# A graph-network kernel on one core: the adjacency build's table of chunk ranges goes from one packed word a block to three plain words

## The reference, cut to what matters

```python
def reference(x, src, dst, edge_attr_8, edge_type_2, edge_weight, ...):
    ei = jnp.stack([src, dst])
    x = ln(x + L0(x, ei, edge_weight))   # segment_sum over ei[0] of (x @ W)[ei[1]] * edge_weight, + bias
    x = ln(x + L1(x, ei, edge_type_2))   # two relational layers, weights mixed from 30 bases, gated
    x = ln(x + L2(x, ei))                # degree-normalized sum over neighbours
    x = ln(x + L3(x, ei, edge_attr_8))   # attention over the edges, 8 heads, bias edge_attr_8
    return x
```

## Time and profile before

| | |
|---|---|
| median of 3 runs | 1315.63 us (1310.06 to 1317.89) |
| the profiled execution | 1321.34 us |
| its span (first to last instruction) | 1319.6 us |
| mean granted clock of PE in it, as a share of full speed | 0.981 |
| PE busy | 1223.5 us (93%) |
| DVE busy | 862.3 us (65%) |
| ACT busy | 419.5 us (32%) |
| POOL busy | 309.3 us (23%) |
| build, first to last matmul of L1600 | 68.7 to 245.9 us |

### The profile page before, as it was taken

One profiled execution on the slowest core, in us unless ns is written; L12 is line 12 of the kernel. 1 busy time (PEld: TensorE's weight loads), 2 busy tenths in 40 slices (PEclk: granted clock), 3 DMA queues, 4 the chain that ended last, 5 costly groups with the idle time before them and its releaser, 6 DMA issues.

```text
span 1319.6 us, 22145 instructions
## 1 busy us (share of the span) xinstructions
PE 1223.5 (93%) x8447; PEld 551.8 (42%) x8448; DVE 862.3 (65%) x1178; ACT 419.5 (32%) x564; POOL 309.3 (23%) x220
## 2 busy tenths in 40 slices
PE   6888888899898999999999999989999899999997
PEld 2233333333343333344445443444332455555553
DVE  7475666344334555462478873646999788879787
ACT  2444555322232111212301002125551343334332
POOL 2011010000010243453555655555560000000000
PEclk9988999999998999999999999989999899999999
DMA  8577885598696888745122212113221665556552
GB/s 305 207 235 237 278 288 181 208 371 323 209 368 213 277 273 265 231 117 159 2 49 33 49 21 46 2 2 42 32 32 53 229 219 193 176 177 201 172 173 104
DMA packets 64267, 222.77 MB, mean 169 GB/s; under 512 B 31208, under 2 KB 36072, under 8 KB 48214
## 3 DMA queue, kind: packets, MB, share of 16 engines
q1 hardware_dynamic: 34648, 156.40, 34.8%
q0 software_dynamic: 25184, 53.10, 15.6%
q10 hardware_dynamic: 4350, 12.07, 2.7%
HBM read 198.94 MB, written 59.94 MB: 196 GB/s over the span
## 4 chain that ended last, share of the span: by engine, by line
PE 47%; DVE 8%; issue 6%; DMA 5%; ACT 1%; SPq 0%; DVEq 0%
PE PS L1716 18%; PE PS L1670 6%; PE PS L1955 5%; PE PS L1942 5%; DMA R<-in_basis_s 4%; DVE R L1108 4%; PE PS L1988 3%; PE PS L1975 2%; PE PS L1837 2%; PE PS L1536 2%; DVE R L1143 1%; PE PS L1752 1%; DVE R L1170 1%; PE PS L1641 1%; DMA W<-w_d 1%
## 5 line engine op out<-in xcount | busy, mean ns | idle before, releaser
L749 POOL DMA_INDIRECT bias_d<-R x160 | 271.4, 1696 | 339.6 <-DMA bias_d<-R 224.0
L1716 PE MATMUL PS<-R 128*128 128x512 f16 x1300 | 301.3, 384 | 1.6 <-DVE R L946 1.6
L1716 PEld LDWEIGHTS PS<-R 128*128 128x128 f16 x1300 | 121.2, 98 | 184.7 <-issue 53.6
L1600 PE MATMUL PS<-R,XX 125*128 125x512 f16 (+2 forms) x612 | 131.6, 349 | 26.4 <-DVE R L863 15.3
L1501 ACT ACTIVATE R<-PS 128x1024 f32<-128x1024 f32 (+1 forms) x100 | 100.5, 1005 | 163.4 <-PE PS L1942 163.4
L1143 DVE SCALAR_TENSOR_TENSOR R<-R,W 128x1024 f32<-128x1024 f32 (+1 forms) x68 | 134.3, 1985 | 14.3 <-ACT R L1501 13.1
L1670 PE MATMUL PS<-W,XX 128*128 128x512 f16 x600 | 135.3, 384 | 4.2 <-DVE R L946 2.7
L863 DVE TENSOR_SCALAR R<-W,R 125x1250 f16<-125x1250 f16 x160 | 89.6, 606 | 47.5 <-PE PS L1600 44.1
L1108 DVE CUSTOM_DVE_ANT_0 R<-PS,R 128x1250 f16<-128x1250 f32 x80 | 116.8, 1460 | 5.5 <-PE PS L1889 2.9
L1955 PE MATMUL PS<-R 128*32 128x256 f32 (+1 forms) x1600 | 105.7, 382 | 5.4 <-DVE R L1143 4.8
L1942 PE MATMUL PS<-R 128*128 128x256 f16 (+3 forms) x800 | 105.9, 274 | 1.1 <-DVE R L1108 1.1
(11 more groups left out here) (220 smaller groups left out, 1361.0 us busy)
## 6 DMA issues: line engine op xcount, KB each, us to landing
bias_d<-bias_d POOLq DMA_DIRECT2D x39, 1280.0 KB, 11.5
R<-in_basis_s SPq DMA_DIRECT2D x48, 1024.0 KB, 6.4
W<-bias_d SPq DMA_DIRECT2D x27, 1024.0 KB, 4.9
R<-bias_d SPq DMA_DIRECT2D x13, 1024.0 KB, 4.8
W<-in_basis_s SPq DMA_DIRECT2D x12, 1024.0 KB, 6.0
R<-key_d SPq DMA_DIRECT2D x20, 500.0 KB, 3.8
R<-R SPq DMA_DIRECT2D x120, 80.0 KB, 6.3
W<-bias_d SPq DMA_DIRECT2D x7, 904.0 KB, 4.6
```

The lines of the kernel that those rows point to most:

```text
L749: pool.indirect_dma_start(bias_d, bass.IndirectOffsetOnAxis(ap=idx[:, c:c + 1], axis=0), attr[:, c, :], None, bounds_check=DUMP + GC * P - ...
L1600: ins = T.matmul(mm_out(3 * (j % 2) + b, p1 - p0), own[0:EC, bass.ds(c, 1), :, :].rearrange("p c m w -> p (c m w)"), hots(p0, p1), start=f ...
L1716: ins = T.matmul(mm_out(SUM_BANK(s, i), D), lhs, rhs, start=n == 0, stop=n == len(terms) - 1)
```

## The change

The table holds three words a block: `lo`, `hi` and `off`. The DVE code that packed them is gone, the DRAM row and the SBUF row are three times as long, and `tile_ranges` loads twelve words a tile instead of four and uses them as they are.

```diff
-        tab_d = dram("tab_d", (1, TT), I32)
+        tab_d = dram("tab_d", (1, 3 * TT), I32)
-        tab = in_w(TT)[0:1, :].bitcast(I32)
+        tab = in_w(3 * TT)[0:1, :].bitcast(I32)
 
         def tile_ranges(eng, t4):
 
-            ap = tab[:, bass.ds(t4 * 4, 4)]
+            ap = tab[:, bass.ds(t4 * 12, 12)]
             _, vals = nc.values_load_multi_w_load_instructions(ap, engines=(eng.engine,), min_val=0,
                                                                 max_val=2 ** 31 - 1)
-            ranges = []
-            for p in vals:
-                first = within((p >> 8) & 255, 0, CH - FIXED - 1)
-                end = within(first + (p & 255) + FIXED, FIXED + 1, CH)
-                ranges.append((first, end, eng.snap(p >> 16)))
-            return ranges
+            return [(within(vals[3 * j], 0, CH - FIXED - 1), within(vals[3 * j + 1], FIXED + 1, CH),
+                     eng.snap(within(vals[3 * j + 2], 0, (TT + 1) * CH)))
+                    for j in range(4)]
 
             sp.wait_ge(tab_out, 1)
-            sp.dma_start(tab_d[0, :].rearrange("(t k) -> t k", k=1), tabi[0:TT, 0:1]).then_inc(tab_out, 16)
+            sp.dma_start(tab_d[0, :].rearrange("(t k) -> t k", k=3), tabi[0:TT, :]).then_inc(tab_out, 16)
 
-            V.tensor_copy(tabi[0:TT, 0:1], bound[0:TT, 0:1])
-            V.tensor_copy(tabi[0:TT, 1:2], lohi[0:TT, 0:1])
-            step(V.tensor_copy(tabi[0:TT, 2:3], visits[0:TT, :]))
-            for k in range(2):
-                step(V.tensor_scalar(tabi[0:TT, 0:1], tabi[0:TT, 0:1], 8, None, ALU.logical_shift_left))
-                step(V.tensor_tensor(tabi[0:TT, 0:1], tabi[0:TT, 0:1], tabi[0:TT, k + 1:k + 2], ALU.bitwise_or))
+            V.tensor_copy(tabi[0:TT, 2:3], bound[0:TT, 0:1])
+            step(V.tensor_copy(tabi[0:TT, 0:2], lohi[0:TT, :]))
             V.tensor_copy(inside[0:TT, 0:1], visits[0:TT, :]).then_inc(tab_out, 1)
```

## The result

The changed kernel takes 1341.12 us (median of 4 runs, 1338.45 to 1344.42), the kernel before 1313.39 us (4 runs): a ratio of 1.021, 95% interval 1.0183 to 1.0236. It is 27.7 us slower. Further down, two executions of the kernel before, of 1864 and 2803 us, lie far above all others, and the ratios leave them out.

The account below looks back on a forecast made before the run. PE, busy 93% of the span, was taken to bound the kernel. Loads and register work summed to + 9.8 us, PE's clock added + 7: + 17 on 1315.6 gave 1333 us, range 1319 to 1344.

Parts of the forecast that it names:

- rival B: The table's wider load is itself slower, 0.7 us more in each of ten tiles: 1340 us, chance 0.15.
- The pairs: FUSED_REGOPS and SEQ_ASSERT after a tile's load: eight more on PE, 0.3 us each and unhidden, 2.3 us a tile.
- TENSOR_LOAD: The table's load at a tile's head, twelve words instead of four: 0, up to + 0.7 us a tile.
- The clock: PE's granted clock falls at seven more heads of the build, 1.0 us each: + 7 us.
- Inside a tile: Less unpacking between blocks of a tile saves 0.28 us in each of 30 blocks until ACT binds: - 8.4 us.
- The first tile: At the build's start PE waits for DVE, whose own load gets eight more pairs, less unpacking: + 1.9 us.
- DVE in later tiles: DVE's load comes 2.3 us later, but its first `hot` stands ready 5.1 us before PE begins: 0.
- Making the table: Before the build, small vector operations go and the DRAM round trip grows; DVE's 16.18 us of idle time covers it: 0.
- The carry behind the build: The stage after the build hangs on its end, so the build's delay is carried on in full.
- Rival A: The clock stays up at the build's heads despite PE's longer idle time: 1325 us, chance 0.22.
- D: Rival: the stage behind the build waits for DMA, not PE, and absorbs the delay: 1318 us, chance 0.09.
- C: Rival: added pairs at a tile's load cost 0.1 us each and no clock falls: - 5 us, 1310, chance 0.04.

Follow-up runs that it names:

- e2: The changed kernel without the check pairs (FUSED_REGOPS and SEQ_ASSERT) on the loaded words, two masks a block instead: 1304.39 us, ratio 0.9914 to the kernel before.
- e9: As e6, but the table has four words a block, the fourth unused, so each load is of four words: 1298.73 us, ratio 0.9877.
- e4: The changed kernel with four matmuls of constants on PE ahead of the table's load in each of the nine later tiles: 1334.86 us, ratio 1.0143.
- e1: The kernel before, but a tile loads and checks twelve words and uses only every third, the packed one, unpacked as before: 1354.61 us, ratio 1.0303.
- e5: The changed kernel, but each block loads its own three words with their check pairs at its own head: 1316.68 us, ratio 1.0008.
- e6: As e5, but without the check pairs and with the two masks a block of e2: 1305.90 us, ratio 0.9925.
- e7: The kernel before with its packed word, but each block loads its own word with its check pair at its own head: 1307.14 us, ratio 0.9929.
- e10: As e9, but PE's loop over the ten tiles is written out in the program; DVE and ACT keep their loops: 1305.87 us, ratio 0.9922.

## Why the prediction was right, and where it was too small

The direction and the range (1319 to 1344) held, and so did the mechanisms that were priced. The size did not: + 27.7 us where + 17 was forecast, since one term was put at nothing and another was too small. The changed kernel landed on rival B's number, 1340, but that is luck: B's longer load is only about 6 of the 11 us that were missing, the clock most of the rest. Going by its own steps, with the build's end 28.4 us later:

| step | forecast, us | measured, us |
|---|---|---|
| idle time at nine heads (load and pairs) | + 18.9 | + 25.1 |
| clock at nine heads, less the shorter loop there | + 5.2 | + 9.5 |
| first tile | + 1.9 | + 2.1 |
| 30 blocks inside tiles, second passes | - 9.2 | - 8.3 |
| sum | + 17 | + 28.4 |

*The pairs: right.* 0.29 us each, bare on PE's path, as e2 showed by taking them away.

*TENSOR_LOAD: the step that failed.* I took 0 "since 362 to 1380 for the same four words says that something other than their number sets it", and kept the 0.7 us a tile as rival B. The wide spread of PE's load said nothing against a dependence; DVE's, 355 ns at the shortest with a median of 358, was the steady row, and I should have asked there. It went to 862 ns. On PE the nine loads at heads grew by 0.72 us each on average (362 to 1057 at the first, 487 to 1059 at the last): that is rival B's price, and it is all that the heads' idle time exceeds the forecast by (9 x 0.7 = 6.3 of 6.2). The upper bound, three times 358 ns, was above what DVE's steady load showed, and the length does not go by words (e9).

*The clock: right in kind, undersized.* It fell at all nine heads, as forecast. I priced a fall at 1.0 us, from one of the two tiles that had one; e4 measures 1.7. In the kernel before, the two heads with a fall, blocks 8 and 12, took 5.2 and 5.4 us from first matmul to `built`, where a head without one takes 3.8: a price of 1.3 and 1.6 us already. But behind both stands a block with a second pass, and these took 4.66 and 4.19 us from `built` to `built`, where block 30, also with a second pass, took 5.32. They gave 0.7 and 1.1 us back, because the idle time ahead of the second pass shrank. The two rows are the second pass of block 13, behind a fall, and that of block 30:

```profile
130.31 0.69 PE L1600 MATMUL PS<-R,XX 125*128 x3 [0.17 <-issue]
...
205.42 0.69 PE L1600 MATMUL PS<-R,XX 125*128 x3 [0.72 <-issue]
```

So the comparison of whole tiles hid about half of what the slow block itself lost, and only two of nine heads have such a block behind them. The rest comes from the heads at 112, 236 and 257 us, where the half clock lasted twice as long as in rows 7 and cost 1.9 to 2.7 us each against e4, the other six 1.0 to 1.7.

*A third stretch at half clock: overlooked.* The prediction says that the clock was at 0.50 in two stretches of the build, behind its longest idle times. The build's first block was at 0.50 as well, behind the longest of all, 4.53 us, and for longer than the other two:

```profile
68.70:73.90 5.20, 5.19 (x16) 2.25 (x17) 4.40 (x9) 0.00 (x0) 0.00 (x0) 0.50 0.00 0
```

It was the one place in the build before with an idle time like those that the change makes.

*Inside a tile: right.* 3.62 us from `built` to `built` where 3.6 was forecast, with the fix 0.05 us behind ACT's copy (206.34 + 1.24 = 207.58, fix at 207.63); e1, with the old register code, is back at 3.9.

*The first tile: right by luck.* DVE's idle time ahead of its first `hot` grew from 2.13 to 5.47 us, not by 1.9, since its first load went from 625 to 1942 ns on top of the pairs. The first matmul came 3.1 us later. But the half clock ended 3.2 us into the first block instead of 5.2, so that this block was 1.0 us shorter, which no term had.

*DVE in later tiles: right at 0.* Its `hot` for block 28 was ready at 209.8, PE began at 214.71. The lead before was 4.5 us and not 5.1, since 190.34 is where that `hot` begins and not where it is ready; it was enough.

*Making the table: right at 0.* DVE still stands idle 15.8 us ahead of the build.

*The carry behind the build: right as far as it can be seen.* DVE's move, SP's load and PE's first mix behind the build all start 28.4 or 28.5 us later, and the medians differ by 27.7. The prediction's last sign, that the span grows by what the last `built` loses, is met less well by the two traces: 23.1 of 28.4 us, within the scatter of what follows. Rival A is out, since the clock fell behind every head. D, under which most of the loss is absorbed, is out by the medians. C is out too: its price of 0.1 us a pair was 0.29.

## What to carry to other kernels

Work of a sequencer costs only where the instructions queued ahead of it run out, so look in the trace for register instructions where an engine's idle time is put down to something that was long done. Before words are unpacked to save shifts, count what each loaded word brings with it. The plain words made this kernel 2% slower at the tiles' heads, left it as it was when they were spread over the blocks with their checks (e5), and made it 1% faster only without the checks (e2, e6, e9). The packed word, spread over the blocks with its one check, was 1% faster as well (e7), so that gain came from moving or removing the checks and not from the plain words. And price an idle time on PE together with what its clock does behind it: here 1.7 us on top of each. Read that price from the block that was slow and from the one behind it, not from a whole stretch that may hide it.

## What the runs showed of the hardware that I had not expected

A TENSOR_LOAD of three words took more than twice as long as one of four: 0.74 to 0.78 us against 0.33 to 0.35 (shortest and median, e6 and e9), on PE and DVE alike.

On PE the same load takes from its shortest to over 1 us more (0.96 to 2.03 us for twelve words in the changed kernel, 0.33 to 1.48 for four in e9), mostly at a tile's head; writing the tiles out removed some of the long ones and not all. What lengthens them stays open, but they have company: in e9, leaving out the first tile, all six loads on PE that are over 15% above the shortest fall into a stretch in which one of SP's store instructions takes over 1.5 us instead of 0.6, and only 5 of the 32 others do; in e10 it is 5 of 6 and 6 of 32. Whether one causes the other, or both have the same cause, no run shows.

How long PE had stood idle did not settle by itself whether its clock fell. In the kernel before it fell behind 1.88 and 2.09 us; in e5 it did not behind 1.83, 1.99 and 2.09 us, and did behind 1.56 us with another 0.39 us soon after. The 1.43 us that brought no fall in the kernel before, twice, had one behind them in e2, where 2.06 us more followed in the same block.
